# Graph layer with own-made gathers: eight-bit pick blocks from ScalarE, and four tiles of both halves fetched by TensorE

## The chip, the core and the metric

The kernel runs on one core of one Trainium2 chip. The metric is the device time of one execution in microseconds (us): the median of the runs, lower is better. Engines are named as in the profile: PE is TensorE (PEld its weight loads), DVE is VectorE, ACT is ScalarE, POOL is GpSimd, SP is SyncE.

## The reference

A relational graph layer with a residual and a layer norm: 3125 nodes of 64 numbers, 103125 edges (sorted by `dst`), 16 relations with a 64 x 64 weight each.

```python
h = feat[src]                                   # one row of x for each edge
def step(m, rw):                                # for each of the 16 relations
    r, w_r = rw
    mask = jnp.where(etypes == r, 1.0, 0.0).astype(h.dtype)
    return m + mask[:, None] * (h @ w_r), None
m, _ = jax.lax.scan(step, m0, (jnp.arange(n_rels), weight))
out = jax.ops.segment_sum(m, dst, num_segments=feat.shape[0])
x = layernorm(x + out)                          # over the 64 numbers of a node
```

## The kernel before

**Tiles, groups, halves.** The edges are cut into 806 tiles of 128. 13 tiles are a group; a turn `i` of the main loop takes two groups, the halves `u = 0` and `u = 1`. There are 31 turns (0 to 30); turns 0, 1 and 30 are written out, the loop holds two turns, an even and an odd one, and runs 14 times.

**Rows of x.** The rows are held as sums of three bf16 parts (192 columns, and the first part once more). For each tile the 128 rows `x[src]` must be brought to `rows`. Most tiles get them by an indirect DMA that POOL issues (`fetch` in the block of POOL, L330). The first tiles of a half are fetched by PE instead (`fetch_own`, L756): a node number is `25 p + b`, and for each of 25 blocks `b` a matrix with a 1 where the edge's source is node `25 p + b` (a pick block, 125 partitions x the tile's 128 edges) is loaded as weights and multiplied with block `b` of `xp`. So a tile is 25 matmuls of 192 columns, summed in PSUM. ACT then copies them to `rows`, two tiles at a time (`take_pair`, L430).

**How many.** `own_count` (L207): four tiles of half 0 in each turn; of half 1 four in odd turns and three (`FEWER`) in even ones, where POOL issues a tenth indirect DMA for the fourth tile (L341).

**Who makes the pick blocks.** DVE makes 20 of 25 with one comparison each (`picks`, L533), over all edges of the half's own tiles at once: 516 columns for four tiles, 384 for three. ACT makes the last five (`APICK`) in two passes each (`act_picks`, L405): `Abs(src - node)` into `away`, then `Relu(1 - away)`. They stand in four parts of 2, 3, 2 and 3 passes, between ACT's other work. The source numbers come by a DMA from SP and are narrowed to fp16 by ACT (`narrow_sources`, L381).

**Aggregation.** `aggregate` (L786) adds the 13 tiles of a half to windows of nodes x relations: 39 matmuls, weights from `rows`, columns from a one-hot that DVE makes (`onehots`). `relate` (L811) multiplies by the relations' weights: 16 matmuls, once in a turn.

**The order of a turn on PE**, which is the order of the code: `fetch_own(i, 1)`, `relate(i - 1)`, `aggregate(i, 0)`, one transpose, `fetch_own(i + 1, 0)`, `aggregate(i, 1)`. Semaphores tie it to the others. A fetch of PE waits for DVE's and ACT's blocks (`pick_ready`, `act_pick_ready`, L759). POOL starts its indirect DMAs of a half when the aggregation before has read `rows` (`agg_ready`) and ACT has written the indices (`gidx_ready`); ACT writes those last in its half of a turn, behind the fourth part of its pick passes:

```python
                take_pair(i + 1, 0, 0, not odd)
                act_picks(i + 1, 1, 1, not odd)
                act_picks(i + 1, 1, 2, not odd)
                take_pair(i + 1, 0, 1, not odd)
                act_picks(i + 1, 1, 3, not odd)
            group_indices(i + 1, 1)
```

**Four stretches.** In the rows and in the prediction, a stretch runs from the first matmul of a fetch of PE to the first of the next one. A: half 1 of an even turn (75 own matmuls, `relate`, `aggregate`). B: half 0 behind it (100 own, `aggregate`). C: half 1 of an odd turn (100 own, `relate`, `aggregate`). D: half 0 behind that (100 own, `aggregate`). A + B + C + D is one pass of the loop.

## Time and profile before

| | before |
|---|---|
| median of 3 runs | 1327.59 us (1325.9 to 1332.8) |
| profiled execution, span | 1331.0 us |
| busy PE, PEld | 905.4 us (68%), 801.7 us (60%) |
| busy DVE, ACT, POOL | 656.1 us (49%), 628.9 us (47%), 553.1 us (42%) |
| mean granted clock of PE | 0.784 of full speed |

The span goes from the first to the last instruction of the one execution that was profiled; no time of its own is given for that execution beside the three runs, and its span lies 3.4 us above their median. A busy share is a mean over stages with different limits. "issue" as the reason of an idle time means that the engine waited for nothing that the profile shows. The granted clock is 1.0 or 0.5 at any moment (2.4 or 1.2 GHz), so a value between is a mix of the two over the stretch.

### The profile page before, as it was taken

What the parts mean: (1) busy time and instruction counts of PE and PEld (TensorE: products, weight loads), DVE (VectorE), ACT (ScalarE), POOL (GpSimd) and SP (SyncE); (2) the same over time, 40 slices, a digit from 0 to 9 for tenths busy, and PEclk for the clock granted to TensorE, in tenths of its full rate; (3) what the DMA queues carried; (4) which work ended last, traced back from release to release, by engine and by line L of the source; (5) the groups of instructions that cost most, each with busy time, mean ns of one, the idle gap of its engine ahead of it and who ended that gap; (6) DMA issues with size and microseconds to landing.
All of it is one profiled execution on the core that took longest, in us unless ns stands there. A gap on an engine that the chain in (4) does not pass through costs nothing.

```text
span 1331.0 us, 25286 instructions
## 1 busy us (share of the span) xinstructions
PE 905.4 (68%) x8746; PEld 801.7 (60%) x8747; DVE 656.1 (49%) x2201; ACT 628.9 (47%) x1217; POOL 553.1 (42%) x591
## 2 busy tenths in 40 slices
PE   4576686766766768676675857667676766767676
PEld 3465575665656657566565756557575655756575
DVE  7653644545545364453635445363544545354444
ACT  6455453553544535444453535445363444535442
POOL 5643534444434353343534344352533435344341
PEclk9687887877868688686887778786787778788676
DMA  6211211111111111111111111121111111111111
GB/s 166 54 45 37 53 40 39 42 46 42 43 36 46 33 51 42 38 45 34 49 40 41 38 41 43 34 51 28 53 41 36 45 34 51 35 44 43 28 28 35
DMA packets 29901, 58.93 MB, mean 44 GB/s; under 512 B 11656, under 2 KB 11906, under 8 KB 29882
## 3 DMA queue, kind: packets, MB, share of 16 engines
q0 software_dynamic: 18464, 37.85, 11.0%
q1 hardware_dynamic: 11264, 20.41, 5.8%
q10 hardware_dynamic: 154, 0.42, 0.1%
q8 instruction: 12, 0.20, 0.1%
q14 instruction: 7, 0.06, 0.0%
HBM read 56.23 MB, written 2.40 MB: 44 GB/s over the span
## 4 chain that ended last, share of the span: by engine, by line
PE 66%; issue 30%; ACT 2%; DVE 1%; DMA 0%; ACTq 0%; DVEq 0%
PE own L767 48%; PE agg L805 11%; PE rel L818 6%; ACT pick L426 1%; DVE outT L647 0%; DMA x_sb<-in_x 0%; ACT away L420 0%; PE rel L825 0%; PE own L915 0%; DVE x_sb L681 0%; ACT rows L436 0%; DVE xp L558 0%; PE own L748 0%; ACT idx L451 0%; DVE outT L622 0%
## 5 line engine op out<-in xcount | busy, mean ns | idle before, releaser
L767 PE MATMUL own<-xp,pick 125*128 125x192 bf16 x5725 | 653.5, 271 | 377.6 <-issue 371.3
L767 PEld LDWEIGHTS own<-xp,pick 125*128 125x128 bf16 x5725 | 545.9, 108 | 474.6 <-issue 458.6
L345 POOL DMA_INDIRECT rows<-x_parts,gidx x558 | 529.5, 949 | 612.5 <-ACT gidx L379 231.1
L539 DVE TENSOR_SCALAR pick<-src_h,node 125x516 bf16<-125x516 f16 (+1 forms) x1220 | 459.7, 456 | 291.5 <-ACT src_h L387 290.3
L435 ACT ACTIVATE rows<-own 128x384 bf16<-128x384 f32 x122 | 57.4, 470 | 643.0 <-remote 581.2
L622 DVE TENSOR_TENSOR outT<-outT,rel 64x32 f32 x124 | 22.3, 180 | 361.6 <-PE rel L825 349.2
L420 ACT ACTIVATE away<-src_h,node_neg 125x516 bf16<-125x516 f16 (+1 forms) x305 | 192.5, 693 | 7.6 <-PE own L767 5.9
L426 ACT ACTIVATE pick<-away,one 125x516 bf16<-125x516 bf16 (+1 forms) x305 | 192.0, 696 | 0.0
L805 PE MATMUL agg<-onehot,rows 128*128 128x112 bf16 x2418 | 167.9, 243 | 15.8 <-issue 15.6
L805 PEld LDWEIGHTS agg<-onehot,rows 128*128 128x128 bf16 x2418 | 163.7, 117 | 18.3 <-issue 18.1
L605 DVE TENSOR_SCALAR onehot<-ramp,krel 128x112 bf16<-128x112 bf16 x806 | 148.9, 262 | 6.6 <-PE agg L805 6.6
L818 PE MATMUL rel<-w_pair,aggT 128*128 128x64 f32 x496 | 88.2, 349 | 9.5 <-issue 9.4
L818 PEld LDWEIGHTS rel<-w_pair,aggT 128*128 128x128 f32 x496 | 86.1, 267 | 12.2 <-issue 12.0
L399 ACT ACTIVATE aggT<-agg 64x512 f32<-64x512 f32 x124 | 73.1, 589 | 25.6 <-PE agg L805 12.5
L341 POOL DMA_INDIRECT rows<-x_parts,gidx x16 | 15.1, 942 | 134.0 <-PE agg L805 72.4
L391 ACT ACTIVATE agg<-zeros 128x1024 f32<-128x1024 bf16 x64 | 65.8, 1028 | 2.0
L387 ACT ACTIVATE src_h<-src_b 125x516 f16<-125x516 int32 (+1 forms) x61 | 36.6, 599 | 0.0
L436 ACT ACTIVATE rows<-own 128x128 bf16<-128x128 f32 x122 | 32.5, 266 | 0.0
L379 ACT ACTIVATE gidx<-idx 128x13 int32 (+1 forms) x62 | 13.0, 209 | 0.0
L748 PE MATMUL own<-ident,src_f 62*128 62x62 f32 x13 | 1.6, 313 | 12.8 <-DVE src_f L560 12.8
L825 PE MATMUL rel<-ident,rel_rows 128*64 128x128 f32 x31 | 9.8, 315 | 0.4 <-ACT rel_rows L443 0.4
L443 ACT ACTIVATE rel_rows<-rel 128x64 f32<-128x64 f32 x31 | 7.0, 226 | 6.3 <-PE rel L818 6.3
(67 smaller groups left out, 83.0 us busy)
## 6 DMA issues: line engine op xcount, KB each, us to landing
src_b<-in_src SPq DMA_DIRECT2D x61, 258.0 KB
rows<-x_parts,gidx POOLq DMA_INDIRECT x577
x_parts<-xp SPq DMA_DIRECT2D x1, 728.0 KB
x_parts<-xp SPq DMA_DIRECT2D x1, 672.0 KB
out<-x_sb SPq DMA_DIRECT2D x2, 224.0 KB
x_sb<-in_x ACTq DMA_DIRECT2D x1, 364.0 KB
x_sb<-in_x SPq DMA_DIRECT2D x1, 336.0 KB
src_i<-in_src SPq DMA_DIRECT2D x1, 312.0 KB
```

The source lines that it names most:

```text
L345: pool.indirect_dma_start(rows[:, u, j, :], None, x_parts, bass.IndirectOffsetOnAxis(ap=gidx[:, u, j:j + 1], axis=0)).then_inc(rows_in[u] ...
L387: act.activation(src_h[u][:, :, 0:w], src_b[u][0:NP, 0:CUT * w].rearrange("p (c w) -> p c w", c=CUT), ACT.Copy, bias=-float(MID)).then_inc ...
L391: act.activation(agg[u][:, :, :], zeros[:, :].rearrange("p (h k) -> p h k", h=2), ACT.Copy).then_inc(agg_copied[u], 1)
L399: act.activation(aggT[q * D:(q + 1) * D, :, u, :], agg[u][q * D:(q + 1) * D, :, :].rearrange("d h (n r two) -> d r (h n) two", r=RQ, two=2 ...
L420: last = act.activation(away[:, b, 0:CUT * cut_width(u, odd)].rearrange("p (c w) -> p c w", c=CUT), src_h[u][:, :, 0:cut_width(u, odd)], A ...
L426: last = act.activation(pick[u][:, VPICK + b, 0:CUT * cut_width(u, odd)], away[:, b, 0:CUT * cut_width(u, odd)], ACT.Relu, bias=one[:, :], ...
L435: act.activation(rows[:, u, 2 * k:2 * k + n, 0:SPLIT * D], pair[:, 0:n, 0:SPLIT * D], ACT.Copy).then_inc(own_rows[u], 1)
L539: v.tensor_scalar(pick[u][:, b, 0:CUT * cut_width(u, odd)], src_h[u][:, :, 0:cut_width(u, odd)], node[:, b:b + 1], None, ALU.is_equal).the ...
L605: last = v.tensor_scalar(onehot[:, u, j, :], ramp[:, :, 0:R], krel[:, bass.ds(i * (2 * GT) + (u * GT + j), 1)], None, ALU.is_equal)
L767: return nc.tensor.matmul(own_slot(u, h), pick[u][:, b, h * P:(h + 1) * P], xp[:, b, 0:SPLIT, :].rearrange("p s d -> p (s d)"), start=(b = ...
L805: last = nc.tensor.matmul(agg[u][:, int(j >= HALF[1]), bass.ds(at[j], KEYS)], rows[:, u, j, s * D:(s + 2) * D], onehot[:, u, j, :], start= ...
L818: last = nc.tensor.matmul(rel[:, 0:D], aggT[:, q, :, :].rearrange("d u n -> d (u n)"), w_pair[:, q, :], start=(q == 0), stop=(q == RQ - 1))
```

## The change

ACT makes 8 of the 25 blocks and DVE 17. ACT does one pass for a block: `1 / sqrt(|8 (src - node) + 15/1024|)`, which is 8.26 where the numbers are equal and under 0.36 elsewhere, written as uint8, so 8 or 0. PE reads these bytes as eight-bit floats, in which the code 8 is 2^-6. DVE's blocks hold 2^-6 too (a second operation, a multiplication, in the same instruction), and ACT multiplies by 64 when it copies the sums to `rows`. `FEWER`, the third-tile case of `own_count` and POOL's tenth DMA are gone: PE fetches four tiles of both halves in every turn. ACT's passes stand in four parts of 2.

```diff
-    FEWER = 3
...
-    APICK = 5
+    APICK = 8
+    STEEP = 8.0
+    NUDGE = 15.0 / 1024.0
+    CODE = 8
+    PICK = 2.0 ** -6
...
-        pick_all = [sb(f"pick{u}", [P, NB * OWNW[u]], bf16) for u in range(2)]
...
-        away = sb("away", [NP, APICK, max(OWNW)], bf16)
-        node_neg = sb("node_neg", [NP, NB])
+        pick_all = [sb(f"pick{u}", [P, VPICK * OWNW[u]], bf16) for u in range(2)]
...
+        code = [sb(f"code{u}", [NP, APICK, OWNW[u]], u8) for u in range(2)]
+        node_off = sb("node_off", [NP, NB])
...
-            return OWN[u] if u == 0 or odd else FEWER
+            return OWN[u]
...
-                if own_count(u, odd) == FEWER:
-                    pool.indirect_dma_start(
-                        rows[:, u, FEWER, :], None, x_parts,
-                        bass.IndirectOffsetOnAxis(ap=gidx[:, u, FEWER:FEWER + 1], axis=0)).then_inc(fourth_in, 16)
...
+            act.preload_act_table(ACT.Abs_reciprocal_sqrt)
...
-                cuts = (0, APICK // 2, APICK)
-                b0, b1 = cuts[part % 2], cuts[part % 2 + 1]
-                if part < 2:
-                    for b in range(b0, b1):
-                        last = act.activation(away[:, b, 0:CUT * cut_width(u, odd)].rearrange("p (c w) -> p c w", c=CUT), src_h[u][:, :, 0:cut_width(u, odd)], ACT.Abs,
-                                              bias=node_neg[:, VPICK + b:VPICK + b + 1])
...
-                    for b in range(b0, b1):
-                        last = act.activation(pick[u][:, VPICK + b, 0:CUT * cut_width(u, odd)], away[:, b, 0:CUT * cut_width(u, odd)], ACT.Relu, bias=one[:, :], scale=-1.0)
...
+                w = cut_width(u, odd)
+                for b in range(part * APICK // 4, (part + 1) * APICK // 4):
+                    last = act.activation(code[u][:, b, 0:CUT * w].rearrange("p (c w) -> p c w", c=CUT), src_h[u][:, :, 0:w],
+                                          ACT.Abs_reciprocal_sqrt, bias=node_off[:, VPICK + b:VPICK + b + 1], scale=STEEP)
...
-                    v.tensor_scalar(pick[u][:, b, 0:CUT * cut_width(u, odd)], src_h[u][:, :, 0:cut_width(u, odd)], node[:, b:b + 1], None, ALU.is_equal).then_inc(pick_ready[u], 1)
+                    v.tensor_scalar(pick[u][:, b, 0:CUT * cut_width(u, odd)], src_h[u][:, :, 0:cut_width(u, odd)], node[:, b:b + 1], PICK, ALU.is_equal, ALU.mult).then_inc(pick_ready[u], 1)
...
+                    hot = pick[u][:, b, h * P:(h + 1) * P] if b < VPICK else code[u][:, b - VPICK, h * P:(h + 1) * P].bitcast(f8)
```

PE, in the loop, half 1 of an even turn (stretch A), from the wait for the blocks to `relate`, before (L767 is the own matmul, L818 `relate`):

```order
L763 ISA [waits act_pick_ready1,pick_ready1]
L767 MATMUL own<-xp,pick 128x192 [waits own_rows1]
L767 MATMUL own<-xp,pick 128x192 x49
L771 ISA
L767 MATMUL own<-xp,pick 128x192 [waits own_rows0]
L767 MATMUL own<-xp,pick 128x192 x24
```

The same place now (L758 is the own matmul):

```order
L753 ISA [waits act_pick_ready1,pick_ready1]
L758 MATMUL own<-xp,pick 128x192 [waits own_rows1]
L758 MATMUL own<-xp,pick 128x192 x16
L758 MATMUL own<-xp,code 128x192 x8
L758 MATMUL own<-xp,pick 128x192 x17
L758 MATMUL own<-xp,code 128x192 x8
L762 ISA
L758 MATMUL own<-xp,pick 128x192 [waits own_rows0]
L758 MATMUL own<-xp,pick 128x192 x16
L758 MATMUL own<-xp,code 128x192 x8
L758 MATMUL own<-xp,pick 128x192 x17
L758 MATMUL own<-xp,code 128x192 x8
```

The fetch has 25 matmuls more, and of each 25 the last 8 read the codes. The waits are the same.

ACT, in the loop, half 0 of the odd turn's fetch (stretch B, the quoted code above), from the first pair of tiles to the indices, before:

```order
L435 ACTIVATE rows<-own 128x2x192 [waits own_done0]
L436 ACTIVATE rows<-own 128x2x64
L420 ACTIVATE away<-src_h,node_neg 125x516 x3
L424 REGISTER_ALU
L426 ACTIVATE pick<-away,one 125x516 [waits away_ready]
L426 ACTIVATE pick<-away,one 125x516
L432 REGISTER_ALU
L435 ACTIVATE rows<-own 128x2x192 [waits own_done0]
L436 ACTIVATE rows<-own 128x2x64
L424 REGISTER_ALU
L426 ACTIVATE pick<-away,one 125x516 [waits away_ready]
L426 ACTIVATE pick<-away,one 125x516 x2
```

And now:

```order
L425 ACTIVATE rows<-own 128x2x192 [waits own_done0]
L426 ACTIVATE rows<-own 128x2x64
L415 ACTIVATE code<-src_h,node_off 125x516 x4
L422 REGISTER_ALU
L425 ACTIVATE rows<-own 128x2x192 [waits own_done0]
L426 ACTIVATE rows<-own 128x2x64
L415 ACTIVATE code<-src_h,node_off 125x516 x2
L381 ISA [waits late_in1]
L381 ACTIVATE gidx<-idx 128x13
```

Between the two pairs there are four passes in place of five, and between the second pair and the indices (`gidx`) two in place of three.

POOL, the half-1 run of an even turn, before:

```order
L341 DMA rows<-x_parts,gidx 128x256 [waits agg_ready1,gidx_ready1]
L345 DMA rows<-x_parts,gidx 128x256 x9
L333 REGISTER_ALU [waits agg_ready0]
L345 DMA rows<-x_parts,gidx 128x256 [waits gidx_ready0]
L345 DMA rows<-x_parts,gidx 128x256 x8
```

And now:

```order
L346 DMA rows<-x_parts,gidx 128x256 [waits agg_ready1,gidx_ready1]
L346 DMA rows<-x_parts,gidx 128x256 x8
L338 REGISTER_ALU [waits agg_ready0]
L346 DMA rows<-x_parts,gidx 128x256 [waits gidx_ready0]
L346 DMA rows<-x_parts,gidx 128x256 x8
```

The run of ten indirect DMAs is a run of nine, as the others are.

## Rows read from the trace of the kernel before

**Rows 1.** The page: busy time of each engine.

```profile
PE 905.4 (68%) x8746; PEld 801.7 (60%) x8747; DVE 656.1 (49%) x2201; ACT 628.9 (47%) x1217; POOL 553.1 (42%) x591
```

**Rows 2.** Timeline of PE: start us, us, what, count, idle before.

```profile
653.38 5.69 PE L767 MATMUL own<-xp,pick 125*128 125x192 bf16 x67 [0.71 <-issue]
...
666.87 4.16 PE L767 MATMUL own<-xp,pick 125*128 125x192 bf16 x26 [0.37 <-issue]
670.87 1.92 PE L818 MATMUL rel<-w_pair,aggT 128*128 128x64 f32 x16
672.63 2.08 PE L805 MATMUL agg<-onehot,rows 128*128 128x112 bf16 x39
```

**Rows 3.** Timeline of POOL: first and last DMA of a run of nine, then of ten.

```profile
654.12 0.94 POOL L345 DMA_INDIRECT rows<-x_parts,gidx  x1 [9.47 <-ACT gidx L379]
...
664.11 0.95 POOL L345 DMA_INDIRECT rows<-x_parts,gidx  x1 [0.30 <-issue]
...
611.36 0.94 POOL L341 DMA_INDIRECT rows<-x_parts,gidx  x1 [9.85 <-PE agg L805]
...
622.59 0.94 POOL L345 DMA_INDIRECT rows<-x_parts,gidx  x1 [0.31 <-issue]
```

**Rows 4.** Timeline of PE in stretch A, behind its own matmuls.

```profile
625.67 3.59 PE L818 MATMUL rel<-w_pair,aggT 128*128 128x64 f32 x16
629.05 3.85 PE L805 MATMUL agg<-onehot,rows 128*128 128x112 bf16 x39
```

**Rows 5.** Stretches: PE, PEld, DVE, ACT, POOL busy, PEclk, DMA share, GB/s.

```profile
610.45:632.90 22.45, 14.88 (x134) 13.46 (x132) 10.19 (x33) 10.45 (x21) 9.43 (x10) 0.70 0.17 41
632.90:653.38 20.48, 13.78 (x140) 12.08 (x139) 10.87 (x37) 9.86 (x19) 8.49 (x9) 0.83 0.16 42
653.38:675.00 21.62, 15.34 (x156) 13.64 (x157) 10.19 (x33) 10.40 (x22) 8.49 (x9) 0.84 0.14 40
675.00:694.72 19.72, 13.18 (x139) 11.29 (x140) 9.46 (x37) 9.22 (x21) 8.48 (x9) 0.83 0.18 43
...
907.20:931.12 23.92, 18.08 (x159) 16.32 (x157) 10.19 (x33) 10.93 (x22) 8.49 (x9) 0.71 0.13 36
```

**Rows 6.** Sums over the 14 stretches of A, B, C and D, in this order.

```profile
sum 303.58, PE 203.78 PEld 183.07 DVE 142.08 ACT 145.37 POOL 132.05; mean PE 14.56 PEld 13.08 DVE 10.15 ACT 10.38 POOL 9.43
...
sum 285.22, PE 192.46 PEld 169.98 DVE 152.16 ACT 138.37 POOL 118.89; mean PE 13.75 PEld 12.14 DVE 10.87 ACT 9.88 POOL 8.49
...
sum 309.90, PE 222.82 PEld 198.94 DVE 142.66 ACT 147.23 POOL 118.86; mean PE 15.92 PEld 14.21 DVE 10.19 ACT 10.52 POOL 8.49
...
sum 280.19, PE 193.93 PEld 169.32 DVE 136.81 ACT 128.66 POOL 118.88; mean PE 13.85 PEld 12.09 DVE 9.77 ACT 9.19 POOL 8.49
```

**Rows 7.** Timeline of ACT: pick passes in B, in C and in D.

```profile
651.34 1.95 ACT L426 ACTIVATE pick<-away,one 125x516 bf16<-125x516 bf16 x3
...
671.62 1.34 ACT L426 ACTIVATE pick<-away,one 125x516 bf16<-125x516 bf16 x2
...
692.86 1.62 ACT L426 ACTIVATE pick<-away,one 125x384 bf16<-125x384 bf16 x3
```

**Rows 8.** Tile gidx: POOL's idle time before its runs, by what ended it.

```profile
  ACT gidx L379: 292.4, 30
  PE agg L805: 280.9, 29
```

**Rows 9.** Timeline, turn 30: PE behind the last stall, and POOL's last DMA.

```profile
1304.59 3.73 PE L805 MATMUL agg<-onehot,rows 128*128 128x112 bf16 x38 [0.45 <-issue]
...
1301.65 0.94 POOL L345 DMA_INDIRECT rows<-x_parts,gidx  x1 [0.30 <-issue]
```

**Rows 10.** Groups of instructions: busy, mean ns of one, idle before.

```profile
L767 PEld LDWEIGHTS own<-xp,pick 125*128 125x128 bf16 x5725 | 545.9, 108 | 474.6 <-issue 458.6 <-DVE pick L539 1.9 <-ACT idx L451 1.8
...
L818 PEld LDWEIGHTS rel<-w_pair,aggT 128*128 128x128 f32 x496 | 86.1, 267 | 12.2 <-issue 12.0
```

**Rows 11.** Timeline of DVE in stretch B.

```profile
634.43 7.87 DVE L539 TENSOR_SCALAR pick<-src_h,node 125x516 bf16<-125x516 f16 x20
```

More of the change, by code:

```diff
@@ L18, in gnn_resnorm @@
     f32, i32, f16, bf16 = mybir.dt.float32, mybir.dt.int32, mybir.dt.float16, mybir.dt.bfloat16
+    u8, f8 = mybir.dt.uint8, mybir.dt.float8e4
     ALU, ACT, AX = mybir.AluOpType, mybir.ActivationFunctionType, mybir.AxisListType
@@ L59, in gnn_resnorm @@
     GAP = 2
-    APICK = 5
+    APICK = 8
[3 more added lines that the diff above has]
+    PICK = 2.0 ** -6
+    assert CODE < NUDGE ** -0.5 < CODE + 0.5 and (STEEP - NUDGE) ** -0.5 < 0.5
     VPICK = NB - APICK
@@ L127, in gnn_resnorm @@
         src_h = [sb(f"src_h{u}", [NP, CUT, CUTW[u] + GAP], f16) for u in range(2)]
-        pick_all = [sb(f"pick{u}", [P, NB * OWNW[u]], bf16) for u in range(2)]
-        pick = [pick_all[u][0:NP, :].rearrange("p (b e) -> p b e", b=NB) for u in range(2)]
-        away = sb("away", [NP, APICK, max(OWNW)], bf16)
-        node_neg = sb("node_neg", [NP, NB])
+        pick_all = [sb(f"pick{u}", [P, VPICK * OWNW[u]], bf16) for u in range(2)]
+        pick = [pick_all[u][0:NP, :].rearrange("p (b e) -> p b e", b=VPICK) for u in range(2)]
+        code = [sb(f"code{u}", [NP, APICK, OWNW[u]], u8) for u in range(2)]
+        node_off = sb("node_off", [NP, NB])
         one = sb("one", [NP, 1])
@@ L220, in cut_width @@
         def cut_width(u, odd):
-            return CUTW[u] if own_count(u, odd) == OWN[u] else FEWER * P // CUT
+            return CUTW[u]
         def own_slot(u, h):
@@ L318, in _ @@
             pool.iota(node[:, :], pattern=[[1, NB]], base=-MID, channel_multiplier=NB,
-                      allow_small_or_imprecise_dtypes=True).then_inc(const_set, 1)
-            pool.iota(node_neg[:, :], pattern=[[-1, NB]], base=MID, channel_multiplier=-NB,
-                      allow_small_or_imprecise_dtypes=True).then_inc(const_set, 1)
+                      allow_small_or_imprecise_dtypes=True).then_inc(node_set, 1)
             pool.memset(one[:, :], 1.0).then_inc(const_set, 1)
+            pool.wait_ge(node_set, 1)
+            pool.tensor_scalar(node_off[:, :], node[:, :], -STEEP, NUDGE, ALU.mult, ALU.add).then_inc(const_set, 1)
             pool.memset(zeros[:, :], 0.0).then_inc(zeros_set, 1)
@@ L335, in fetch @@
                 if not has_own(i, u):
-                    for j in range(FEWER):
+                    for j in range(OWN[u]):
                         pool.indirect_dma_start(
@@ L434, in take_pair @@
                 n = min(2, own_count(u, odd) - 2 * k)
-                act.activation(rows[:, u, 2 * k:2 * k + n, 0:SPLIT * D], pair[:, 0:n, 0:SPLIT * D], ACT.Copy).then_inc(own_rows[u], 1)
-                act.activation(rows[:, u, 2 * k:2 * k + n, SPLIT * D:RP * D], pair[:, 0:n, 0:D], ACT.Copy).then_inc(own_rows[u], 1)
+                act.activation(rows[:, u, 2 * k:2 * k + n, 0:SPLIT * D], pair[:, 0:n, 0:SPLIT * D], ACT.Copy, scale=1.0 / PICK).then_inc(own_rows[u], 1)
+                act.activation(rows[:, u, 2 * k:2 * k + n, SPLIT * D:RP * D], pair[:, 0:n, 0:D], ACT.Copy, scale=1.0 / PICK).then_inc(own_rows[u], 1)
             def take_rel(i):
@@ L445, in _ @@
             narrow_sources(0, 0, False)
-            act.wait_ge(const_set, 5)
+            act.wait_ge(const_set, 4)
             act_picks(0, 0, 0, False)
@@ L750, in edge_transposes @@
                 last.then_inc(done, 1)
-            pe.wait_ge(const_set, 5)
+            pe.wait_ge(const_set, 4)
             pe.wait_ge(src_cast, 1)
@@ L766, in product @@
                 def product(h, b):
-                    return nc.tensor.matmul(own_slot(u, h), pick[u][:, b, h * P:(h + 1) * P],
+                    hot = pick[u][:, b, h * P:(h + 1) * P] if b < VPICK else code[u][:, b - VPICK, h * P:(h + 1) * P].bitcast(f8)
+                    return nc.tensor.matmul(own_slot(u, h), hot,
                                             xp[:, b, 0:SPLIT, :].rearrange("p s d -> p (s d)"), start=(b == 0), stop=(b == NB - 1))
@@ L795, in aggregate @@
                 else:
-                    pe.wait_ge(first_in, 16 * FEWER)
+                    pe.wait_ge(first_in, 16 * OWN[u])
                 for j in range(GT):
-                    if j == FEWER and own_count(u, odd) == FEWER:
-                        pe.wait_ge(fourth_in, (i // 2 + 1) * 16 if isinstance(i, int) else (i + 2) * 8)
                     if j == OWN[u]:
```

20 lines of the change are left out of this document (6 added, 14 removed).

## The prediction

> **What bounds the kernel now.** I read the page first, then PE's timeline over one pass of the loop, POOL's and ACT's beside it, the stretches as windows, and last what ends POOL's idle time. On the page no engine is full: PE is busy 68% and the others under 50% [rows 1]. So a sum of busy times forecasts nothing, and the reader should look for what repeats in a stretch. One pass of the loop is four stretches, 22.45 + 20.48 + 21.62 + 19.72 = 84.27 us [rows 5]; over all 14 passes the mean is (303.58 + 285.22 + 309.90 + 280.19) / 14 = 84.21 us [rows 6]. That is 1179 of the 1331.0 us of the span.
>
> In stretch C the first 67 own matmuls take 5.69 us, 85 ns each. Then, for 7.8 us, single ones go by, and at 666.87 us, 13.5 us into the stretch, the last 26 start; they take 4.16 us, 160 ns each [rows 2]. PE waits for no named engine in between. What ends the wait stands in POOL's timeline: its run of nine indirect DMAs goes from 654.12 to 665.06, an interval of 1.25 us, and PE resumes 1.81 us behind its end. In stretch A the run has ten and goes from 611.36 to 623.53, and PE is through at 625.67, 2.14 us behind [rows 3, 4]. I take this as the frame: a stretch is the start of POOL's run, 10.94 us for nine DMAs (12.17 for ten), about 1.85 us, and what PE still has to do. The granted clock has fallen in the stall: in C the 26 matmuls run at the low level, 160 ns against 85, and `relate` and `aggregate` behind them at the high one (1.92 and 2.08 us), whereas in A these two run at the low one, 3.59 and 3.85 us [rows 2, 4]. The trace doesn't say why PE stalls beside POOL; only the regularity is used here.
>
> POOL's run in turn starts when the aggregation is over and ACT has written the indices: of 59 waits 30 were ended by ACT's indices and 29 by PE's aggregation [rows 8].
>
> **The change part by part.**
>
> The tile and the tenth DMA (stretch A, 14 in the loop and one behind it). The 25 matmuls more are 2.1 us at 85 ns or 4.0 us at 160 ns. They don't simply add: 75 own matmuls were done within the stall, so PE then stood with only `relate` and `aggregate` left, and the stall was a DMA, 12.17 - 10.94 = 1.23 us, longer. With four tiles and nine DMAs stretch A becomes what C is now: the same instructions on PE, POOL and ACT. Typical A is 22.45 and typical C 21.62 us, -0.83 [rows 5]. The means over 14 are 303.58 / 14 = 21.68 and 309.90 / 14 = 22.14, +0.45 [rows 6], because three C stretches in fourteen (as 907.20 to 931.12, clock 0.71 in place of 0.84) take 23.9 us. The term for 14 stretches is thus +6.3 us by the means, -11.6 by the typical rows. Both ends are kept.
>
> ACT's chain to the indices (ends of B, C, D). Behind the second pair of tiles come two passes in place of three. Three take 1.95 us in B and two of the same take 1.34 in C, so one is 0.61 us [rows 7]. No row shows a pass with the new function into uint8. Lower bound: an `Abs` or `Relu` pass as it is, 0.61; upper bound: the two passes that it stands for, 1.22. I take 0.61, since source, columns and the form with a bias pointer are those of `Abs`. The Trainium skill ("ScalarE: Activation LUTs", section "ACT is a hardware spline evaluator") says one element per cycle and lane whatever the function; by it the pass is 0.61 too, and no run here shows it yet. The indices then come 0.61 us earlier. But the aggregation stays where it is. It ends at 672.63 + 2.08 = 674.71 in C, against a next stretch at 675.00 [rows 2, 5]; and where nothing but it is waited for, as at the end of A (629.05 + 3.85 = 632.90, the start of B [rows 4, 5]), the next stretch starts at its end. So C can give 0.29 at most, and I take 0.23, as POOL's start has its own delay behind the aggregation. B gives all 0.61: its wait before the next fetch is 0.71 us [rows 2]. D now ends with three passes of 384 columns, 1.62 us, and will end with two of 516, 1.34: 0.28 [rows 7]. The new A is as C, 0.23. Were every end bound by ACT: 14 x (0.61 + 0.23 + 0.28 + 0.23) = 18.9 us. Only 30 of 59 are [rows 8]: 30 x 0.37 (mean of B, C and D), and ten of A's fourteen x 0.23, is 11.2 + 2.3 = 13.5 us. Ends: -13.5 and -18.9.
>
> The last pair. Turn 30's fetch had 75 matmuls, and behind POOL's last DMA (1302.59) and the stall only `aggregate` was left, 3.73 us [rows 9]. Now some 26 own matmuls (4.16) and `relate` (1.92) [rows 2] come behind a run that ends 1.23 earlier, and `aggregate` at 2.08: 4.16 + 1.92 - 1.23 - 1.65 = +3.2 us.
>
> Costed at nothing. DVE: 20 comparisons are 7.87 us, 0.393 each [rows 11]; 17 are 6.7. If the second operation cost it double, 17 would be 13.4 us; with the one-hots it ends some 17 us into a stretch of 20, so the rest of the stretch still covers it; bound 0 to +3 us in the start-up, where DVE's blocks are waited for. Start-up itself: two passes and three comparisons fewer, -1 us. PE's codes: 8 of 25 weight loads read bytes. Lower bound the bf16 load, 108 ns, which hides under the next matmul; upper bound the dearest load here, 267 ns in fp32 [rows 10], that is 0.16 x 8 of each 25, for the 26 matmuls behind the stall 1.3 us a stretch. I take nothing: as many columns and fewer bytes. ACT's multiplication by 64 rides in a copy that is made anyway. The copy of A's third and fourth tile is one of 384 columns in place of 192, inside what C has.
>
> **The sum**, against the span of 1331.0 us. By means: +6.3 - 13.5 + 3.2 - 1 = -5. By typical rows, all ends bound by ACT: -11.6 - 18.9 + 3.2 - 1 = -28.3. What lies between is how often the clock rises late; the granted clock is 0.84 in one C and 0.71 in another, for the same work [rows 5], and nothing shows which of the two a shorter stretch will get, so neither end has a claim. I take the middle, -16: 1315 us of span, and with the 3.4 us between span and median 1311.6, say **1312 us**. Its own range is 1299 to 1322.
>
> **The rivals.**
>
> *More than that* (0.14). Shorter stretches put the resume so that the clock rises sooner everywhere; C and the new A never take 23.9. Three C stretches at 21.6 are 7 us more than the sum by typical rows: 1327.6 - 28.3 - 7 = 1292. For it: the late ones were at clock 0.71 and lasted 2.3 us longer for the same counts. Against: no row shows that they go away.
>
> *Nothing to be measured* (0.17). The earlier resume is spent at the low clock, where it buys half: of 13.5 us some 7 stay, and the tile costs its +6.3 + 3.2. Sum +2 to -5: 1323 to 1330.
>
> *The tile is not covered; slower* (0.08). If PE's stall isn't tied to POOL's run but to what PE itself has issued since the fetch began (in both A and C it comes after some 67 matmuls), then nine DMAs in place of ten free nothing, and 25 more matmuls add to A at the clock behind the stall: 15 x 4.0 = 60 us, or 15 x 2.1 = 31 us at the high one. With ACT's 13.5 back: 1327.6 + 31 - 13.5 = 1345 to 1374. For it: the count of 67. Against: PE resumes 1.8 to 2.1 us behind POOL's last DMA in both. It decides once A takes over 23.4 us. The Trainium skill ("TensorE: Matmul & The Clock Gate", "Back-to-back issue gap") counts a matmul's columns at the clock plus 2.5 ns, 82.5 ns for 192; by that rule alone 375 more matmuls are 31 us, the low end of this rival; the 85 ns of the trace agree with the gap, and the stall is what the rule leaves out.
>
> *A pass into uint8 with the new function is dear; slower* (0.04). At 1.22 us two passes are 2.56 with the first one's start (1.34 + 1.22), against 1.95: each of four ends in a pass of the loop comes some 0.6 later, 14 x 2.4 = +34, and with 3 off for the tile 1327.6 + 34 - 3 = 1359. The forecast's 16 us are gone when the four ends come 16 / 14 = 1.14 us later than forecast in a pass, 0.29 each by two passes: at 0.61 + 0.14 = 0.75 us a pass it decides.
>
> *The codes load slowly* (0.02): 59 x 1.3 = +77 us, 1390 at most.
>
> **How the numbers follow.** The forecast has 0.55, the others 0.14, 0.17, 0.08, 0.04 and 0.02. 0.5% of 1327.6 is 6.6 us, which is about what a measurement of this kernel can tell from no change: 1321.0 to 1334.2. The forecast's range reaches a little into it, so faster 0.68, same 0.19, slower 0.13. The range of 8 in 10 takes in the larger gain and the case without any, and leaves the slower ones out: 1292 to 1331.
>
> **What would show it.** Own matmuls 6100; runs of nine DMAs alone; POOL's last DMA to PE's resume 1.8 us in all four stretches; A at 21 to 22 us; B near 19.9 and D near 19.5; a code pass 0.61 us behind the one ahead; more of POOL's waits ended by PE's aggregation than by ACT's indices. It is wrong if A grows by more than 1 us, if B doesn't shrink, or if a load of codes takes over 108 ns.

## The result and the profile after

The changed kernel takes 1303.74 us (median of 4 runs, 1303.25 to 1304.14), the kernel before beside it 1326.74 us (4 runs, 1323.08 to 1332.8): a ratio of 0.983, 95% interval 0.980 to 0.987. So it is 23.0 us faster. The profiled spans are further apart, 1302.2 against 1331.0 us, -28.8, because the profiled run of before is the longest of its runs (1332.8 us, 6 us above the median). So the stretches compared below give together some 6 us more than the medians do, and no run tells in which of them.

The page of the changed kernel, busy time of each engine, stands against [rows 1]. PE has 375 more matmuls and is busy 4.5 us less; VectorE has lost 51 us, ScalarE 54 and POOL 14.

```profile
PE 900.9 (69%) x9121; PEld 793.4 (61%) x9122; DVE 605.4 (46%) x2018; ACT 575.3 (44%) x1095; POOL 539.5 (41%) x576
```

The four stretches of one pass, the columns as in [rows 5], and the sums over the 14 stretches of A, B, C and D as in [rows 6]:

```profile
602.90:624.38 21.48, 15.60 (x157) 13.91 (x158) 9.02 (x30) 9.25 (x19) 8.51 (x9) 0.84 0.16 40
624.38:643.77 19.39, 13.32 (x142) 11.38 (x139) 9.70 (x34) 8.78 (x18) 8.51 (x9) 0.82 0.18 44
643.77:665.20 21.43, 15.48 (x157) 13.69 (x157) 9.02 (x30) 9.44 (x20) 8.51 (x9) 0.84 0.15 40
665.20:684.76 19.56, 13.25 (x142) 11.43 (x139) 9.68 (x34) 8.93 (x18) 8.51 (x9) 0.83 0.18 44
...
sum 300.84, PE 216.33 PEld 194.14 DVE 125.64 ACT 129.85 POOL 119.15; mean PE 15.45 PEld 13.87 DVE 8.97 ACT 9.28 POOL 8.51
...
sum 270.60, PE 186.20 PEld 159.74 DVE 135.85 ACT 123.00 POOL 119.20; mean PE 13.30 PEld 11.41 DVE 9.70 ACT 8.79 POOL 8.51
...
sum 300.88, PE 216.85 PEld 193.73 DVE 126.31 ACT 132.34 POOL 119.21; mean PE 15.49 PEld 13.84 DVE 9.02 ACT 9.45 POOL 8.52
...
sum 273.09, PE 185.67 PEld 160.62 DVE 139.23 ACT 124.98 POOL 119.20; mean PE 13.26 PEld 11.47 DVE 9.94 ACT 8.93 POOL 8.51
```

By the sums A has given 2.7 us, B 14.6, C 9.0 and D 7.1, together 33.5. The last fetch gives 3.2 back, and the first stretches 1.5: in the timelines of PE the first A begins at 110.57 us before and at 112.02 after, the last fetch at 1289.46 and 1257.43. -33.5 + 1.5 + 3.2 = -28.8, which is the distance of the spans. What the windows show beside it is how even the loop has become. Thirteen of the 14 A have clock 0.84, where the A of before have 0.69 to 0.78. No C is of the kind that stood in the last row of [rows 5]; the longest of 14 is 21.8 us. The D of clock 0.74 to 0.76, eight of 14 before, are gone too: all 14 have 0.82 or 0.83.

The timeline of PE in stretch A, behind POOL's run, against [rows 4], and the first and the last DMA of that run of nine.

```profile
616.69 2.93 PE L758 MATMUL own<-xp,pick 125*128 125x192 bf16 x17
619.41 1.34 PE L758 MATMUL own<-xp,code 125*128 125x192 bf16 x8
620.59 1.92 PE L807 MATMUL rel<-w_pair,aggT 128*128 128x64 f32 x16
622.35 2.08 PE L794 MATMUL agg<-onehot,rows 128*128 128x112 bf16 x39
```

```profile
603.45 0.95 POOL L346 DMA_INDIRECT rows<-x_parts,gidx  x1 [8.15 <-ACT gidx L381]
...
613.46 0.95 POOL L346 DMA_INDIRECT rows<-x_parts,gidx  x1 [0.30 <-issue]
```

The last three code matmuls of the third tile go at 616.25, 1.8 us behind the run (it ends at 613.46 + 0.95 = 614.41), and the 25 own matmuls of the fourth tile stand behind them. These 25 cost 3.9 us, from 616.69 to 620.59, and `relate` and `aggregate` take 3.4 us less than in [rows 4] (3.8 us to the end of the stretch in place of 7.2), since they now run at the high level of the clock. With a run that is one DMA shorter, 25 matmuls more make this A no longer.

POOL's idle time by what ended it, against [rows 8]:

```profile
  PE agg L794: 318.0, 30
  ACT gidx L381: 229.6, 28
```

### The profile page after: what moved, and what is told of

It reads as the page before. It is cut to its first block, busy times and chain, and to the rows that moved or that the text cites. A ratio compares the mean times of both kernels' runs of the same rounds, so it can differ in the third digit from the quotient of the medians.

```text
span 1302.2 us, 25559 instructions
## 1 busy us (share of the span) xinstructions
PE 900.9 (69%) x9121; PEld 793.4 (61%) x9122; DVE 605.4 (46%) x2018; ACT 575.3 (44%) x1095; POOL 539.5 (41%) x576
## 4 chain that ended last, share of the span: by engine, by line
PE 66%; issue 30%; ACT 2%; DVE 1%; another core or an unknown queue 1%; DMA 0%; ACTq 0%; DVEq 0%
PE own L758 53%; PE agg L794 8%; PE rel L807 4%; ACT code L415 1%; DVE outT L637 0%; DMA x_sb<-in_x 0%; PE own L904 0%; PE rel L814 0%; DVE x_sb L671 0%; DVE xp L548 0%; PE own L738 0%; ACT rows L426 0%; ACT idx L441 0%; DVE sqsum L727 0%
## 5 line engine op out<-in xcount | busy, mean ns | idle before, releaser
L758 PE MATMUL own<-xp,pick 125*128 125x192 bf16 x4148 | 479.8, 275 | 86.2 <-issue 79.5
L529 DVE TENSOR_SCALAR pick<-src_h,node 125x516 bf16<-125x516 f16 x1037 | 408.9, 473 | 277.7 <-ACT src_h L389 275.1
L758 PEld LDWEIGHTS own<-xp,pick 125*128 125x128 bf16 x4148 | 406.8, 109 | 130.3 <-issue 118.0
L758 PE MATMUL own<-xp,code 125*128 125x192 bf16 x1952 | 290.1, 273 | 283.0 <-issue 282.4
L758 PEld LDWEIGHTS own<-xp,code 125*128 125x128 fp8e4 x1952 | 190.5, 108 | 344.4 <-issue 339.9
L415 ACT ACTIVATE code<-src_h,node_off 125x516 uint8<-125x516 f16 x488 | 322.9, 721 | 10.9 <-remote 9.3
L794 PE MATMUL agg<-onehot,rows 128*128 128x112 bf16 x2418 | 135.5, 218 | 9.8 <-issue 9.8
L794 PEld LDWEIGHTS agg<-onehot,rows 128*128 128x128 bf16 x2418 | 131.6, 102 | 10.0 <-issue 9.9
L807 PE MATMUL rel<-w_pair,aggT 128*128 128x64 f32 x496 | 64.3, 286 | 0.0
L389 ACT ACTIVATE src_h<-src_b 125x516 f16<-125x516 int32 x61 | 38.2, 626 | 0.0
```

The source lines that it names most:

```text
L389: act.activation(src_h[u][:, :, 0:w], src_b[u][0:NP, 0:CUT * w].rearrange("p (c w) -> p c w", c=CUT), ACT.Copy, bias=-float(MID)).then_inc ...
L415: last = act.activation(code[u][:, b, 0:CUT * w].rearrange("p (c w) -> p c w", c=CUT), src_h[u][:, :, 0:w], ACT.Abs_reciprocal_sqrt, bias= ...
L529: v.tensor_scalar(pick[u][:, b, 0:CUT * cut_width(u, odd)], src_h[u][:, :, 0:cut_width(u, odd)], node[:, b:b + 1], PICK, ALU.is_equal, ALU ...
L758: return nc.tensor.matmul(own_slot(u, h), hot, xp[:, b, 0:SPLIT, :].rearrange("p s d -> p (s d)"), start=(b == 0), stop=(b == NB - 1))
L794: last = nc.tensor.matmul(agg[u][:, int(j >= HALF[1]), bass.ds(at[j], KEYS)], rows[:, u, j, s * D:(s + 2) * D], onehot[:, u, j, :], start= ...
L807: last = nc.tensor.matmul(rel[:, 0:D], aggT[:, q, :, :].rearrange("d u n -> d (u n)"), w_pair[:, q, :], start=(q == 0), stop=(q == RQ - 1))
```

## The experiments

Several chips are behind these runs; the kernel before took 1327 to 1328 us on some and 1352 to 1354 us on others. So every kernel is told by its ratio to the kernel before on its own chip; 0.01 is 13 us. The changed kernel was timed on the 1327 us kind alone, with a ratio of 0.981 to 0.983. On the other kind its ratio is not known and may be lower: experiment 6 has a kernel there that is the changed one with more work, at 0.961. Experiments 1 to 4 and 6 ran on the 1353 us kind, the kernels of experiment 5 on the other, but for its last one. Where this bears on a size, it is said.

### 1. The tile alone

Edit to the kernel before: all that makes A different goes; ScalarE keeps five blocks in two passes each, no codes.

```
-            return OWN[u] if u == 0 or odd else FEWER
+            return OWN[u]
-            return CUTW[u] if own_count(u, odd) == OWN[u] else FEWER * P // CUT
+            return CUTW[u]
```

> The kernel before with four tiles fetched by PE in every turn and no tenth indirect DMA; ACT keeps five blocks in two passes. Theory R (the stall ends with POOL's run): stretch A becomes as C, 21.4 to 22.1 us, so the whole stays within 1318 to 1336 us, near no change, and PE resumes 1.8 us behind POOL's last DMA in A too. Theory N (the stall hangs on what PE has issued): 15 x 2.1 to 15 x 4.0 us more, 1358 to 1387 us.

Measured: ratio 1.011 (1.009 to 1.013), slower by 1.1%. POOL's idle time by what ended it, and the sum over 14 stretches of A:

```profile
  ACT gidx L375: 624.9, 59
```

```profile
sum 311.52, PE 216.88 PEld 193.56 DVE 143.75 ACT 145.40 POOL 118.84; mean PE 15.49 PEld 13.83 DVE 10.27 ACT 10.39 POOL 8.49
```

Neither theory had this: R wanted at most 0.6% more, N at least 2.3%. PE does come back 1.9 us behind a run of nine, as R says; 31 own matmuls are left behind the stall there, against 28 in the changed kernel's A. Against [rows 6] the sums are A +7.9 us, B +8.1 (293.33), C -1.8 (308.12) and D +15.4 (295.60); this is the kind of chip on which the kernel before, too, takes 25 us more, so they don't tell where the 1.1% lies. All 59 waits of POOL end with ScalarE's indices, none with PE's aggregation. The picks for the wider A, made in D, are passes of 516 columns in place of 384; three of these are 1.95 in place of 1.62 us [rows 7], 4.6 us over 14 D. That ScalarE's chain is what costs is borne out by experiment 5, where the same kernel with one pass moved loses far less; by how much the kind of chip adds to it is not shown.

### 2. The codes alone

Edit to the changed kernel: `FEWER` and the tenth DMA come back, so that half 1 of even turns makes three tiles.

```
-            return OWN[u]
+            return OWN[u] if u == 0 or odd else FEWER
```

> The changed kernel with three tiles again in half 1 of even turns and POOL's tenth DMA there. If ACT's shorter chain gives what the prediction says: 11 to 19 us off the kernel before, 1308 to 1316 us; stretch A back at 21.7 to 22.4, B near 19.9. If the two parts add up, its gain and that of the tile alone sum to the 23 us of the whole change; if not, the rest is the clock, which rises at another place when both are made.

Measured: ratio 0.987 (0.985 to 0.989), as expected. The window of one stretch A:

```profile
112.80:134.86 22.06, 14.84 (x132) 13.21 (x132) 9.02 (x30) 9.33 (x19) 9.43 (x10) 0.69 0.18 42
```

With its ten DMAs and 75 matmuls A stays at clock 0.69 to 0.72 in 12 of 14, and 45 of POOL's 59 waits end with PE's aggregation, 14 with ScalarE's indices. In the tile alone A had 0.84 or 0.85 in 6 of 14 and 0.77 or 0.78 in the others; with both parts it is 0.84 in 13. The parts don't add: +1.1% and -1.3% would be -0.2%, and both together have -1.7%, on the other kind of chip. My reading is that the tile takes A out of the low clock but waits for ScalarE, and that the codes take ScalarE out of the way but leave A at the low clock; no run separates the clock from the rest.

### 3. POOL's run of five

Edit to the changed kernel: from the second turn on, the rows of tiles 6 to 9 are not fetched, and PE reads what lies there.

```
-                for j in range(OWN[u], GT):
+                for j in (range(OWN[u], GT) if is_first(i) else (OWN[u], OWN[u] + 1) + tuple(range(LATE, GT))):
```

> The changed kernel, but from turn 1 on POOL issues five indirect DMAs for a half in place of nine (tiles 6 to 9 keep the rows of turn 0, so the sums are other ones). Theory R: PE resumes 1.8 us behind a run that is 4 x 1.25 = 5.0 us shorter, in 59 stretches, so some 280 us less, 1000 to 1050 us. Theory N: PE stalls as before and as long, 1290 to 1305 us. A third theory, D, that the stall hangs on DVE's work beside it (which also ends near 11 us into a stretch): as N.

Measured: ratio 0.723 (0.719 to 0.727). POOL's last DMA of a run and PE's resume, from the timeline of each, and the sum over 14 stretches of A:

```profile
622.01 0.94 POOL L346 DMA_INDIRECT rows<-x_parts,gidx  x1 [0.30 <-issue]
...
624.47 1.49 PE L758 MATMUL own<-xp,code 125*128 125x192 bf16 x8
```

```profile
sum 221.20, PE 192.92 PEld 184.67 DVE 126.32 ACT 130.03 POOL 66.11; mean PE 13.78 PEld 13.19 DVE 9.02 ACT 9.29 POOL 4.72
```

PE is back 1.52 us behind the end of the shorter run, 8.2 us into the stretch. A is (300.84 - 221.20) / 14 = 5.7 us shorter, and four DMAs at 1.25 us are 5.0. Theory N is out: PE had issued the same 63 to 67 matmuls and didn't stand until 13.5 us. So is theory D: VectorE makes one-hots until 625.95, 1.5 us longer than PE stands. In size R fell short: two runs with a median of 977.5 us stand against 1000 to 1050. The stretches are shortened by more than the run, and the granted clock is 0.895 over the span.

### 4. The tenth DMA given back

Edit to the changed kernel, half 1 of even turns alone:

```
+                    pool.indirect_dma_start(
+                        spare[:, :], None, x_parts,
+                        bass.IndirectOffsetOnAxis(ap=gidx[:, u, 3:4], axis=0)).then_inc(spare_in, 16)
```

> The changed kernel with a tenth indirect DMA again in half 1 of even turns, of the fourth tile's rows into a tile that nothing reads. Theory R: stretch A is 1.25 us longer, 15 of them, +19 us, and more (to +35) if the clock then rises late in some stretches: 1320 to 1340 us. Theory N: nothing, 1301 to 1307 us.

Measured: ratio 1.004 (1.002 to 1.005), the changed kernel having 0.983 on its chips. The windows of an A and of the B behind it, the sum over 14 stretches of A, and the timelines of that A: POOL's last DMA ends at 642.31 and PE is back at 644.41.

```profile
629.41:651.72 22.31, 14.77 (x156) 13.33 (x157) 9.02 (x30) 9.28 (x19) 9.44 (x10) 0.85 0.17 41
651.72:672.37 20.65, 14.34 (x142) 12.51 (x139) 9.71 (x34) 8.99 (x18) 8.49 (x9) 0.75 0.15 41
...
sum 321.60, PE 221.26 PEld 198.18 DVE 126.29 ACT 131.21 POOL 132.07; mean PE 15.80 PEld 14.16 DVE 9.02 ACT 9.37 POOL 9.43
```

```profile
641.37 0.94 POOL L354 DMA_INDIRECT rows<-x_parts,gidx  x1 [0.30 <-issue]
...
644.69 2.59 PE L766 MATMUL own<-xp,pick 125*128 125x192 bf16 x15
```

PE is back 2.1 us behind the run's end here, not 1.8. The first pair of A is taken 15.1 us into the stretch in place of 13.4, 1.7 us later for one DMA of 1.25. Over 14 A it is 20.8 us more than in the changed kernel, 1.5 each. B has no DMA more and is still 1.3 us longer than the changed kernel's, at clock 0.75 in place of 0.82, so a part of the price may fall behind A; the two kinds of chip leave that open. On one chip stand this kernel and the codes alone, 1357.1 and 1336.2 us: they differ in the tile and the wider passes for it, with the tenth DMA kept in both, and that costs 20.9 us, 1.4 for each of 15. So a tile costs about what the DMA costs that the change takes off POOL.

### 5. The changed kernel again, and the cut of ScalarE's passes

Three kernels ran on one chip with the changed one. The first of them:

> The changed kernel unaltered, so that the three that follow have it on the same chip. Both theories expect the ratio of before: 0.983 (0.980 to 0.987). Another value would mean that the gain itself depends on the chip, and then the parts (tile alone 1.011, codes alone 0.987, with the tenth DMA 1.004) are compared with the new one.

Measured: 1303.65 us, ratio 0.981 (0.978 to 0.984). The sums over 14 stretches come out the same again: A 301.36, B 271.99, C 301.50 and D 273.05 us.

The last part, behind which the indices come, one pass longer:

```
-                for b in range(part * APICK // 4, (part + 1) * APICK // 4):
+                cuts = (0, 2, 4, 5, APICK)
+                for b in range(cuts[part], cuts[part + 1]):
```

> The changed kernel with ScalarE's eight passes cut 2, 2, 1 and 3 in place of 2, 2, 2 and 2: nothing is added, the last part, behind which the indices come, is one pass of 0.61 us longer. Theory P (the wait for the indices behind ScalarE's last part is what ends each stretch, and what the codes gained): all four stretches of a pass end later, A and C, whose last part ends with PE's aggregate, by the whole 0.61 us, B and D, whose last part ends 0.36 us ahead of the next stretch, by 0.25 to 0.61 us, so 14 to 15 passes give 25 to 36 us and the clock takes its own share: ratio to the changed kernel 1.018 to 1.03, 1.00 to 1.013 to the kernel before. Theory Q (the gain comes from ScalarE's and VectorE's smaller load, wherever it lies): same load, so no more than 1.003 to the changed kernel.

Measured: 1342.14 us, ratio 1.009 (1.005 to 1.012), 1.028 to the changed kernel. POOL's waits:

```profile
  ACT gidx L381: 574.2, 56
```

One pass of 0.61 us moved behind the pair, nothing added, costs 38 us, more than the whole change gave. It is theory P's upper end. But it doesn't lie where P put it: against the sums above D pays 17.8 us, B 10.6, A 9.5 and C 2.1.

One pass shorter, `cuts = (0, 3, 5, 7, APICK)`:

> The changed kernel with the passes cut 3, 2, 2 and 1: the last part is one pass of 0.61 us shorter. Theory P: A and C get back what PE waits for them, 0.1 to 0.3 us each, B and D nothing, since PE's aggregate ends them: 3 to 9 us less, ratio to the changed kernel 0.993 to 0.998; it would then beat both kernels. Theory Q: no change, 0.999 to 1.001. If the first part of three passes holds up the copy of the pair behind it, it is slower instead.

Measured: 1303.53 us, ratio 0.979 (0.976 to 0.982): no difference from the changed kernel. POOL's waits are now all ended by PE:

```profile
  PE agg L795: 559.5, 58
```

```profile
610.88:632.63 21.75, 15.94 (x160) 14.10 (x158) 9.03 (x30) 9.57 (x19) 8.51 (x9) 0.76 0.17 39
```

This A is no shorter than the changed kernel's 21.48, with the indices no longer in its way. The profiled execution is the longest of seven (1312.9 us), so its total says little; in the pass of this A, B and D are 19.15 and 19.26 us, 0.2 to 0.3 shorter than in the changed kernel, and A and C (21.86) 0.3 and 0.4 longer, at clock 0.76 and 0.77 in place of 0.84. In this pass the clock takes what the indices give. So the changed kernel sits where the two chains meet, and of the three cuts tried its 2, 2, 2 and 2 is as good as the best.

The tile alone with the cut moved from 2 and 3 to 3 and 2, `cuts = (0, APICK // 2 + 1, APICK)`:

> The kernel of the tile alone (five picks of ScalarE in two passes each, no codes, ratio 1.011 to the kernel before) with the cut of its passes moved from 2 and 3 to 3 and 2: the same ten passes, the last part 1.33 us in place of 1.95. Theory P: in that kernel all 59 waits of POOL end with ScalarE's indices while PE's aggregate ends 0.3 to 0.7 us before the next stretch begins; taking 0.61 us off the last part gives back 0.3 to 0.6 us in each of 58 stretches, 17 to 35 us, ratio to the kernel before 0.985 to 0.998, that is most of the distance to the changed kernel without any code. Theory Q: the load is unchanged, so 1.009 to 1.013 stays.

Measured: ratio 1.003 (1.001 to 1.006), where the tile alone had 1.011 on the other kind of chip. That is a gain of about 0.8%, less than P wanted. The timeline of ScalarE behind the second pair of A shows why:

```profile
633.06 1.95 ACT L422 ACTIVATE pick<-away,one 125x516 bf16<-125x516 bf16 x3
...
635.01 1.34 ACT L422 ACTIVATE pick<-away,one 125x516 bf16<-125x516 bf16 x2
```

In A and C both of the last parts stand behind the second pair: five passes, however they are cut, and four with the codes. My expectation counted the last part alone. The sums agree, as far as they can be compared across the kinds of chip: against the tile alone B is 19.5 us shorter and D 16.2, A and C only 2.6 and 2.1. The same cut in the kernel before:

> The kernel before with the cut of ScalarE's passes moved from 2 and 3 to 3 and 2, the same ten passes. Behind the last pair of B and D stand then two passes in place of three, behind that of A and C still five. Theory P (the wait for the indices behind ScalarE's last part is what the codes shortened): B's and D's stretches end with PE's work instead, 0.2 to 0.5 us earlier where POOL's wait ended with the indices (30 of 59 waits), 5 to 12 us in all, ratio 0.991 to 0.996; the rest of the gain of the changed kernel over this one is then the fifth pass behind the pair of A and C, and the tile. Theory Q (the load counts): 0.999 to 1.002.

Measured: ratio 0.994 (0.992 to 0.997). So some 0.6% is to be had by moving one pass, without codes or tile. The codes alone had 0.987 on this kind of chip, and their sums are shorter by 4.1 us in C and 5.1 in D, the same in A and 2.4 longer in B. The fifth pass that the codes take away can be C's part of this; it isn't shown, and in A it brought nothing.

### 6. A pause in POOL's run

By now the stall was the largest thing in the trace: PE stands nearly still for 7 us of each stretch while POOL issues DMAs. These kernels leave nothing out; they add work to POOL between its fifth and sixth DMA.

```
+                    if j == OWN[u] + 5:
+                        if not is_first(i) or u:
+                            pool.wait_ge(spare_set, i * 2 + u)
+                            pool.nop(nofuse=True)
+                        pool.memset(spare[:, :], 0.0).then_inc(spare_set, 1)
```

With `spare` of 1024 columns, 0.96 us:

> The changed kernel with a memset of GpSimd over 1024 columns of a spare tile (0.95 us by the row of the zeros) between the fifth and the sixth DMA of every run: 62 runs, nothing else. PE stands nearly still from some 5.7 us of a stretch until 1.8 us behind the run's end. Theory R (PE stands as long as POOL issues its DMAs, and a run that ends later moves PE's return by as much): every stretch is 1.0 to 1.1 us longer, 55 to 68 us in all, ratio to the kernel before 1.02 to 1.035. Theory S (PE comes back in any gap that is long enough and takes its work up there): the gap here is shorter than the 1.8 us that PE's return took, so S gives nearly the same, at least 1.01; a ratio under 1.0 would say that PE comes back faster than that.

Measured: 1302.72 us, ratio 0.961 (0.959 to 0.964). Both theories wanted it slower. The run ends 0.8 us later, yet the first pair is taken 13.6 us into A, against 13.4 in the changed kernel: PE's single matmuls behind the pause are more, and it is back sooner behind the run. 1302.7 us is what the changed kernel takes on the other kind of chip. Whether the pause gains or costs nothing can't be said without the changed kernel on that chip: if it had 0.983 there too, the pause gains 2%; if it had 0.961, the tenth DMA of experiment 4 costs 4%.

With 3072 columns:

> The same with 3072 columns, 2.8 us of GpSimd by three times that row. Theory R in its strict form: every stretch 2.9 to 3.1 us longer, 165 to 185 us in all, ratio to the kernel before 1.105 to 1.12. Theory S: PE comes back 1.4 to 1.8 us into the gap and issues the rest of its 25 to 33 own matmuls in what is left of it and behind it, so that the part behind the run's end is up to 3.8 us shorter, and the stretch comes out between 1 us shorter and 1.5 us longer: 0.94 to 1.05; own matmuls of 0.15 us each would stand inside the gap in the trace of PE, and the first pair would be taken ahead of the run's end.

Measured: 1047.0 us (1045.04 to 1048.72), ratio 0.772 (0.770 to 0.775). The kernel that only waits longer in between is 23% faster than the one before. Timelines of POOL and PE in one stretch B, the pause in the middle:

```profile
511.26 0.94 POOL L352 DMA_INDIRECT rows<-x_parts,gidx  x1 [0.30 <-issue]
512.04 0.24 PE L764 MATMUL own<-xp,pick 125*128 125x192 bf16 x1 [1.01 <-issue]
512.19 2.68 POOL L351 MEMSET spare<- 128x3072 bf16 x1
513.45 0.41 PE L764 MATMUL own<-xp,pick 125*128 125x192 bf16 x3 [1.17 <-issue]
513.70 0.82 PE L764 MATMUL own<-xp,code 125*128 125x192 bf16 x8
514.35 1.57 PE L764 MATMUL own<-xp,pick 125*128 125x192 bf16 x17
515.04 0.95 POOL L352 DMA_INDIRECT rows<-x_parts,gidx  x1 [0.16 <-issue]
515.76 0.82 PE L764 MATMUL own<-xp,code 125*128 125x192 bf16 x8
516.46 1.94 PE L800 MATMUL agg<-onehot,rows 128*128 128x112 bf16 x36
```

PE comes back 1.26 us into the memset and issues 72 matmuls in one go, own ones and most of the aggregate, on to 3.5 us behind the memset's end while POOL is at its DMAs again; then single ones go by as before. All of it is at the high level of the clock, 81 to 88 ns from one own matmul to the next, where the same 25 took 3.9 us in the changed kernel's A. The window of this B, and the sum of the pass from it to the end of the next A:

```profile
505.66:520.83 15.17, 11.03 (x140) 10.14 (x141) 10.88 (x36) 9.33 (x18) 11.16 (x10) 1.00 0.23 58
sum 64.97, PE 50.99 PEld 47.16 DVE 37.49 ACT 36.77 POOL 44.67; mean PE 12.75 PEld 11.79 DVE 9.37 ACT 9.19 POOL 11.17
```

A pass is 64.97 us where the changed kernel's was 81.86, with the same DMAs and 4 x 2.68 us of memsets.

With 2048 columns, 1.82 us:

> The changed kernel with the memset between the fifth and the sixth DMA of GpSimd's runs at 2048 columns, about 1.8 us, between the 0.96 us that moved the ratio to 0.961 and the 2.68 us that moved it to 0.772. In the trace with 2.68 us PE came back 1.26 us into the memset and then issued 28 own matmuls and a part of the aggregate, on to 1.4 us behind the memset's end. Theory S1 (what PE needs is that POOL's queue of DMAs pauses for some 1.3 us; once back it goes on for a while of itself): the same work is done in a pause that is 0.85 us shorter, stretches are up to 0.85 us shorter than with 2.68 us, 50 us in all at most: ratio 0.735 to 0.775. Theory S2 (what PE can issue grows with the pause that is left behind its return): 0.5 us of pause is left in place of 1.4, so a third of the work: the ratio lies between, 0.80 to 0.92.

Measured: 1067.78 us, ratio 0.789 (0.786 to 0.791): between what S1 and S2 wanted, in neither's range, and slower than with the longer pause. Timelines in one stretch A:

```profile
502.14 1.82 POOL L351 MEMSET spare<- 128x2048 bf16 x1
503.38 0.41 PE L764 MATMUL own<-xp,pick 125*128 125x192 bf16 x3 [1.16 <-issue]
...
504.28 2.88 PE L764 MATMUL own<-xp,pick 125*128 125x192 bf16 x17
```

PE comes back just as soon, 1.24 us in, but here the 17 own matmuls take 2.88 us, against 1.57 above: the low level. And 51 of POOL's 58 waits end with ScalarE's indices, against 27 of 57 in the kernel with 2.68 us. Whether a pause between the two, another place for it, or a third pair of passes moved ahead is better still was not tried.

The trace of the kernel before had such pauses already, without any instruction for them. In an A and a D of the loop POOL's third DMA comes late:

```profile
278.29:296.08 17.79, 12.56 (x131) 11.18 (x132) 10.19 (x33) 10.18 (x21) 9.42 (x10) 0.78 0.22 52
...
282.28 0.94 POOL L345 DMA_INDIRECT rows<-x_parts,gidx  x1 [1.20 <-issue]
...
278.29 6.36 PE L767 MATMUL own<-xp,pick 125*128 125x192 bf16 x75 [0.52 <-ACT pick L426]
...
511.17 0.95 POOL L345 DMA_INDIRECT rows<-x_parts,gidx  x1 [0.78 <-issue]
...
507.43 7.01 PE L767 MATMUL own<-xp,pick 125*128 125x192 bf16 x83 [0.18 <-issue]
```

POOL pauses for 1.20 and 0.78 us in place of 0.30. In the A, PE goes on without a stop through all 75 own matmuls, `relate` and 9 of the aggregate, 100 in all; in the D it issues 83, where 65 to 67 are the rule. The A takes 17.79 us (the other 13 have 21.4 to 22.5), the D 18.06. Another D, with a pause of 0.77 us, takes 19.04 (the other 12 have 19.6 to 21.1). So it isn't the memset that lets PE go on, and a pause ahead of the stall, of 0.5 to 0.9 us more than usual, spared 1 to 4 us. Why POOL paused there is not shown; the codes alone have it in the same turn, 1.20 us and an A of 17.85. A pause put behind the second DMA was not tried.

## Why the prediction was right, and where its sizes were off

The forecast was 1312 us in a range of 1292 to 1331, faster at 0.68; 1303.7 was measured, 0.6% below. The mechanism held: the tile is covered, and ScalarE's shorter chain gives the gain. The sizes of the two terms were off. The sum's low end, -28.3, is close to the distance of the spans, -28.8, but by chance: it has -11.6 for the tile and -18.9 for ScalarE's ends, and A gave 2.7 us in all, the other three stretches 30.7. By the medians the gain is 23.0 us.

**The frame** (run, 1.85 us, the rest of PE's work) held in the changed kernel: PE is back 1.80 to 1.84 us behind the run in all four stretches of the pass shown. A run four DMAs shorter brings PE back 5 us sooner and one DMA longer 1.7 us later (experiments 3 and 4), so in this frame the stall belongs to the run. What the frame lacked: it isn't the run's length but that nothing interrupts it (experiment 6).

**The tile** was put at +6.3 to -11.6 us, before ScalarE's share of A, 2.3 to 3.2. The sums give -2.7 for A with both, so the tile itself is near zero, inside the range and near neither end. Both ends were badly read. The "typical" A of 22.45 us is the longest of the 14; the medians are 21.99 for A and 21.81 for C, which makes -2.5 us over 14. And the mean of A holds the one of 17.79 us with POOL's pause, which the changed kernel doesn't have: the other 13 gave 6.4 us, and that one cost 3.7. That the tile costs nothing hangs on the codes: without them it is +1.1% (experiment 1). I had the two as terms of one sum, with 0.23 us of ScalarE at A's end; they aren't independent.

**ScalarE's chain** was put at 13.5 to 18.9 us, of which B 8.5 at the most, C 3.2 and D 3.9. B gave 14.6, C 9.0 and D 7.1. This is the term that was too small. In B one thing was overlooked: before, 28 own matmuls stood behind the stall,

```profile
646.49 4.27 PE L767 MATMUL own<-xp,pick 125*128 125x192 bf16 x28 [0.38 <-issue]
```

and after it is 17 and 8:

```profile
638.18 2.91 PE L758 MATMUL own<-xp,pick 125*128 125x192 bf16 x17
640.90 0.85 PE L758 MATMUL own<-xp,code 125*128 125x192 bf16 x8
```

So ScalarE takes the second pair 0.48 us sooner, 17.41 us into B in place of 17.89, and with the pass of 0.61 that is the 1.09 us by which this B is shorter (20.48 to 19.39); the mean of B is 1.04. Why PE gets three matmuls further in the stall is not shown. In C some 7 us are the three stretches of 23.9 that the changed kernel doesn't have; the other eleven gave 0.16 each, against 0.23 forecast. In D it is alike: the D of [rows 5], at clock 0.83, gave 0.16 (19.72 to 19.56) against 0.28 forecast. The rest comes from the D of clock near 0.75, 20.4 to 21.1 us long, that went away, less 1.9 us for the two short ones with a pause. That is the rival "more than that", which had 0.14: it named the C, not the D. It came true together with a smaller part of the rest than it assumed, and the time lies between it and the forecast.

**A pass into uint8** was taken at 0.61 us. The group of 488 code passes has a mean of 721 ns, against 721 for `Abs` and 724 for `Relu` before, which is one alone; a part of four in a row takes 2.56, so each further one is 0.61. The Trainium skill ("ScalarE: Activation LUTs", section "ACT is a hardware spline evaluator") has one element a cycle whatever the function, and the trace agrees in this: the new function has the 721 ns of `Abs`. The rival of the dear pass is out. Its price was right in size, though: it had 34 us for ends 0.6 us later, and in experiment 5 one pass more at each end cost 38 us.

**Loads of codes** were costed at nothing. Groups of weight loads: 108 ns with codes, 109 without, against 108 in [rows 10].

```profile
L758 PEld LDWEIGHTS own<-xp,pick 125*128 125x128 bf16 x4148 | 406.8, 109 | 130.3 <-issue 118.0 <-ACT idx L441 1.8 <-DVE pick L529 1.1
L758 PEld LDWEIGHTS own<-xp,code 125*128 125x128 fp8e4 x1952 | 190.5, 108 | 344.4 <-issue 339.9 <-ACT code L415 0.7
```

**VectorE's second operation** costs nothing: 17 comparisons with it take 6.70 us in stretch B, 0.394 each, against 0.393 in [rows 11].

**The last pair** was put at +3.2 us and is +3.2: from the last fetch to the end of the span, 44.8 us against 41.5. That is luck: `relate` and `aggregate` are at the low level there, 3.56 and 3.71 us where 1.92 and 2.08 were put, and 13 own matmuls are left behind the stall, not 26. **The start-up** was put at -1 and is +1.5. In the second trace of the same kernel (experiment 5) the first A begins at 108.77 us, over 3 us sooner than in the first, so these traces don't show its sign.

**The slower rivals.** The tile that isn't covered fell with experiment 3. What came nearest to a loss was none of them: the tile alone, slower by ScalarE's chain. Of the signs that I had named, A at 21 to 22 us and D near 19.5 were right, B (19.3, not 19.9) shrank more, and POOL's waits are ended by PE's aggregation 30 times and by ScalarE 28, a thin majority that shows little.

## What to carry to other kernels

Where two chains end each stretch within 0.3 us of each other, cost the parts of a change together: here one alone lost 1.1%, the other alone won 1.3%, and one pass moved to a worse place cost more than the whole change gave. Look at all the stretches of a trace and not at a typical one: the shortest A of the kernel before held the pause that is worth most here. And where an engine shows idle time that no named engine ends, don't take its regularity for a law: change what runs beside it. Here a pause of 1.8 or 2.7 us in POOL's run of indirect DMAs, on top of the change, took the kernel to 0.79 and 0.77 of the time before, where the change by itself had 0.98 on the other kind of chip.
